# A sequence block with a mixture of experts on one core: VectorE's two products of a block pair, in front of the second scan of a slot

## What is computed

```python
x = x + mamba(layernorm(x))          # in_proj -> conv(4) -> silu -> delta, B, C
                                     # h = h * exp(delta * A) + (delta * xc) * B, per token
                                     # y = sum_n h * C + xc * D;  y * silu(z) @ out_proj
x = x + experts(layernorm(x))        # top 2 of 8: silu(x @ w1) * (x @ w3) @ w2
```

## Time and profile before

| | |
|---|---|
| median of 3 runs | 4781.84 us (4776.21 to 4798.81) |
| the profiled execution: its time | 4794.05 us |
| its span, first to last instruction | 4792.3 us |
| first scan of step 0 | 95.5 us after the span's start |
| steps 0 to 2 end at, tile steps 3 to 14 end at | 518.7 us, 2526.3 us |
| busy in the span: PE, DVE, ACT, POOL | 88%, 52%, 39%, 36% |
| VectorE's products L1213 and L1218 | 91 each, mean 410 and 421 ns |

### The profile page before, as it was taken

The page is one execution under the profiler, slowest core; times in us unless marked ns, Lnnn a source line. Parts: engine busy times, 40 slices in busy tenths (PEclk is TensorE's granted clock), DMA queues, the critical chain, the costliest instruction groups (busy, mean ns, idle before and its releaser), DMA issues. The chain is left out here.

```text
span 4792.3 us, 73789 instructions
## 1 busy us (share of the span) xinstructions
PE 4208.5 (88%) x25764; PEld 3403.0 (71%) x25764; DVE 2471.3 (52%) x3377; ACT 1872.3 (39%) x3912; POOL 1706.9 (36%) x1233
## 2 busy tenths in 40 slices
PE   5777888888887988888887499999999999999999
PEld 4555667666666766666676288887888878888787
DVE  3999988888888888888889300000000000000000
ACT  6676765666566566657655100000000000000000
POOL 3667655665665566466555200000000000000000
PEclk8788989989999989999898699999999999999999
DMA  3112443444344344434433221303030303112210
GB/s 135 67 37 84 139 146 102 150 142 153 108 151 146 102 151 141 156 105 150 146 115 119 88 77 19 102 13 105 14 109 13 105 13 104 18 38 80 82 37 16
DMA packets 289412, 452.63 MB, mean 94 GB/s; under 512 B 15862, under 2 KB 183414, under 8 KB 280822
## 3 DMA queue, kind: packets, MB, share of 16 engines
q1 hardware_dynamic: 273078, 412.71, 26.2%
q0 software_dynamic: 14768, 34.41, 3.8%
q10 hardware_dynamic: 1296, 2.37, 0.1%
HBM read 920.96 MB, written 45.95 MB: 202 GB/s over the span
## 5 line engine op out<-in xcount | busy, mean ns | idle before, releaser
L539 POOL TENSOR_TENSOR hs<-hs,bc 128x1024 f32<-128x1024 f32 x512 | 1218.6, 2381 | 448.6 <-DVE hs L1089 426.8
L1089 DVE TENSOR_TENSOR_SCAN hs<-dA,pU 128x1024 f32<-128x1024 f32 x512 | 1168.6, 2282 | 31.8 <-ACT dA L629 9.8
L629 ACT ACTIVATE dA<-delta,aneg 128x255 f32<-128x255 f32 x2048 | 847.6, 507 | 39.2 <-DVE hs L1089 33.9
L947 PE MATMUL pY<-ident,hs 128*128 128x128 f32 x4096 | 573.6, 293 | 310.3 <-POOL hs L539 310.1
L1514 ACT ACTIVATE gate<-pA 128x512 f32<-128x512 f32 x216 | 117.4, 544 | 1861.0 <-PE pB L1556 1861.0
L1556 PE MATMUL pA<-xT,w1s 128*128 128x128 f32 x6048 | 800.6, 275 | 0.7 <-ACT xT L1527 0.7
L1556 PE MATMUL pB<-xT,w3s 128*128 128x128 f32 x6048 | 799.9, 275 | 0.0
L1429 POOL DMA_INDIRECT out<-ow,trow x54 | 84.4, 1562 | 1971.2 <-DVE ow L1651 1971.2
L947 PEld LDWEIGHTS pY<-ident,hs 128*128 128x128 f32 x4096 | 503.0, 151 | 395.6 <-POOL hs L539 301.9
L1556 PEld LDWEIGHTS pA<-xT,w1s 128*128 128x128 f32 x6048 | 741.8, 192 | 26.4 <-issue 25.3
L1556 PEld LDWEIGHTS pB<-xT,w3s 128*128 128x128 f32 x6048 | 737.3, 192 | 0.0
(11 more groups left out here) (197 smaller groups left out, 3267.1 us busy)
## 6 DMA issues: line engine op xcount, KB each, us to landing
w1s<-in_w SPq DMA_DIRECT2D x165, 1024.0 KB
w3s<-in_w SPq DMA_DIRECT2D x165, 1024.0 KB
w2s<-in_w SPq DMA_DIRECT2D x165, 1024.0 KB
ew<-in_w SPq DMA_DIRECT2D x273, 512.0 KB, 4.4
win<-in_w_in SPq DMA_DIRECT2D x128, 512.0 KB, 3.9
bc<-bc_d SPq DMA_DIRECT2D x64, 1024.0 KB, 11.5
w1s<-in_w SPq DMA_DIRECT2D x55, 512.0 KB
w3s<-in_w SPq DMA_DIRECT2D x55, 512.0 KB
```

Source lines behind the costliest of these rows:

```text
L539: pool.tensor_tensor(hs[b][:, :, :], hs[b][:, :, :], bc[:, N + g * PN:N + (g + 1) * PN, :], ALU.mult)\
L629: e = act.activation(dA[k % NB][:, i, 1:T], delta[:, c, 1:T], ACT.Exp, scale=aneg[:, c, n:n + 1])
L947: m = pe.matmul(pY[c % 2][:, t * P:(t + 1) * P], hs[k % NB][:, i, t * P:(t + 1) * P], ident[:, :], start=g == 0 and i == 0 and t == 0, sto ...
L1089: dve.tensor_tensor_scan(hs[b][:, :, :].rearrange("p n t -> p (n t)"), dA[b][:, :, :].rearrange("p n t -> p (n t)"), pU[:, :, :].rearrange ...
```

## The change

The two products of a block pair, with their waits for the tanh and between each other, are issued at position g = 2 of their slot and not at g = 1. That is one number:

```diff
                 def expert(u, g):
 
                     j = u - UP0 - 1
-                    if 0 <= j < ROUNDS and g == 1:
+                    if 0 <= j < ROUNDS and g == 2:
                         ge(dve, e_tanh, ROUNDS * jt + j + 1)
                         dve.scalar_tensor_tensor(eth[:, :, :], eth[:, :, :], 1.0, pEup[:, 0, :, :], ALU.add, ALU.mult)\
                            .then_inc(e_half, 1)
```

## The result

The changed kernel took 4802.89 us (median of 9 runs, 4790.73 to 4810.71), the kernel before 4786.13 us (9 runs, 4776.21 to 4798.81). The ratio is 1.0028, with a 95% interval of 1.0014 to 1.0041: 13 us slower, 7 to 20. That is under the 0.5% named in the prediction, and outside of zero. The profiled execution took 4802.79 us (span 4801.0).

What follows compares the result with a forecast made beforehand. VectorE bounds steps 0 to 2; in tile steps VectorE and TensorE take turns. Per tile step -0.7 + 2.4 = +1.7 us, times 12 +20 us on the median of 4781.84: 4802 us, range 4776 to 4822.

Steps and rivals of the forecast that it cites:

- the part without the clock: Slot 8, per tile step: at full clock TensorE's next block pair would start 0.7 us earlier.
- the clock term: TensorE after its pause in slot 8: 4.8 us of half clock, 2.4 us lost per tile step.
- Slot 8 carries it all: Only slot 8's moved products cost time; the other slots count 0, with 0.3 us as upper end for slot 7.
- The late products: Slot 8: products wait behind the square root and end 4.9 us later; TensorE stands still for 7.8 us.
- The path behind e8 to L887: Slot 8: ScalarE's table load, tanh and copy, 1.95 us, then the turn of 0.65 us: 2.6 us.
- The table load: ScalarE's load in slot 8's critical piece counted without the skill's drain, which would add 1.3 us, 16 us in sum.
- carried unchanged to the end of the step: The +1.7 us per tile step arising in slot 8 lasts to the step's end, times 12: +20 us.
- L1167 was to wait longer: VectorE's waits at L1145 and L1167 grow by about what the tanh waits lose, plus the step's loss.
- The tanh waits: VectorE's idle for the tanh in the tile steps falls from 84.7 us to about 45, counted as no gain.
- VectorE as the bound: Rival: waits at L1145 and L1167 shrink too in the tile steps; 41 us faster, 4741; chance 0.09.
- The harmless pause: Rival: slot 8's pause costs no clock beyond the old order's loss; 8 us faster, 4774; chance 0.12.
- The slower side: Rival: TensorE's block pair in slot 8 at half clock throughout, loses 3.67 us; 36 us slower, 4818; chance 0.29.

Runs made afterwards that it cites:

- experiment 3: Changed kernel plus 14 unread matmuls on TensorE in slot 8, before its wait for the products, steps 3 to 14: 4780.69 us, 0.9989 of the kernel before.
- the filler of slot 12: Kernel before with the reciprocal moved behind slot 8's second scan, plus 6 unread TensorE matmuls in slot 12: 4717.06 us, ratio 0.9852.
- the filler in slot 0: Kernel before with the reciprocal moved behind slot 8's second scan, plus 14 unread TensorE matmuls in slot 0: 4744.20 us, ratio 0.9912.
- experiment 1: Changed kernel with slot 8's pair of products alone put back at g = 1: 4791.13 us, ratio 1.0000 to the kernel before.

## Why the prediction was right, point by point

**The time.** 4802 was forecast and 4802.89 measured. Part of this closeness is luck: against the 4781.84 us of the first three runs the forecast step is +20 us, and the measured ratio is worth +13, with 7 to 20 in the interval. And the right sum has terms that missed in opposite ways, as the next points show: the part without the clock was put too low, the clock term a little too high, and a gain of 1.1 us later in the step was not seen.

**Slot 8 carries it all.** This is shown from both sides, by the pair put back (1.0000) and by the pair moved alone (1.0040).

**The late products.** The forecast put the end of the products 2.4 us behind the root and the pause at 7.8 us. They are 2.3 us (939.92 to 942.25) and 7.84 us. The path behind e8 to L887 was put at 2.6 us and is 3.1 (947.83 to 950.95): ScalarE's load began 0.3 us after TensorE's end, and the turn took 0.85 us, not 0.65. That is why the sum without the clock came out at -0.7 us and the column to L887 of experiment 3 shows -0.2.

**The clock term.** Half clock for 4.8 us and a loss of 2.4 us were taken from the longest pause. In step 5 it was 3.9 us, and e8 lost 5.53 - 3.67 = 1.9 us; in the mean of the twelve steps it lost 2.2. That this term makes the loss is shown by the filler. The Trainium skill's "TensorE: Matmul & The Clock Gate", Part 1, puts the ramp penalty under 1% of a typical kernel span and advises against fitting a specific count of cold matmuls. The clock behind the pause of slot 8 is worth 0.4% here, within that size, but to leave the term out on that ground would have given no loss at all. The prediction read more into it than it says: that sentence of the Trainium skill is on the warm-up at a kernel's start, and its Part 1 counts the cost each time where pauses recur.

**The table load.** The load at 948.10 took 1.28 us, and the tanh began 1.29 us after its start: no drain of 1.38 us stands behind it, as in the earlier trace rows, and the tanh begins 1.56 us after TensorE's end of e8, so none stands ahead of it either. The Trainium skill's "ScalarE: Activation LUTs", section "What ACT_TABLE_LOAD costs", gives 1.28 us for the load and 1.38 for the drain, 2.66 for a switch. The trace agrees with the first and not with the sum.

**What failed** is half of one step: "carried unchanged to the end of the step". It was carried to L701 except for 0.2 us, but the stretch from L701 to L1167 took 15.78 us instead of 16.90. The projection behind the pause at the turn is the place, in step 5:

```profile
994.35 1.22 PE L932 MATMUL pY<-xc,skip 128*128 128x256 f32 x2 [3.16 <-ACT ysum L641]
...
995.79 4.43 PE L827 MATMUL pM<-xnT,win 128*128 128x256 f32 x16
```

The same 16 matmuls took 5.93 us before, behind a pause of the same 3.16 us. In the mean of the twelve steps they took 5.34 us before and 4.23 after, which is the 1.1 us. The half clock lasted less long. With the filler of slot 12 the stretch is 15.14 us, so the half clock cost 1.8 us in it before and 0.6 after. Why it was shorter stays open. In steps 4 to 13 of the changed kernel it goes with e8: in the six steps where e8 took 5.30 to 5.76 us the projection took 4.33 to 4.56, and in the four where e8 took 6.27 to 6.29 it took 3.62, which is full clock throughout. In the kernel before there is no such link. The stretch is short in the four kernels whose products of slot 8 stand at g = 2 (15.78, 15.99, 16.02, 16.10) and long in the three with g = 1 and no filler (16.90, 16.63, 16.70; with the filler in slot 0 it is 16.35), but each has one profile, and no run here tells a cause. It goes with the one waiting time that went against the forecast: L1167 was to wait longer, and waits 6.7 us instead of 17.9.

**The tanh waits** fell to 63.8 us and not to about 45. Slot 5 (13.5 us in the twelve steps, then 0) and most of slot 10 (18.1, then 3.7) went as worked out. The wait of slot 11 was to lose 1.4 us a step and grew instead, from 49.8 to 54.9 us, in step 5 from 3.69 to 5.24 where 2.3 was expected. One part of that is e10 itself, which ran partly at half clock in six of the twelve steps (in three of the kernel before):

```profile
966.24 0.66 PE L913 MATMUL pS<-ident,xb 128*128 128x128 f32 x4 [0.84 <-ACT xnT L695]
966.71 5.36 PE L810 MATMUL pE<-xf,ew 128*128 128x128 f32 x32
```

In step 5 it took 3.57 us to the next work before (956.84 to 960.41) and 5.20 here (966.71 to 971.91); the granted clock over these stretches is 1.00 and 0.67. The rest is that e10 starts later against VectorE's scans, 3.18 us behind the start of the last one before it (963.53) where it was 1.70 (955.14 to 956.84). The prediction had counted neither. With slot 8's pair put back (experiment 1), where e10 takes 3.57 us throughout, the tanh waits are 48.8 us, near the forecast. As the wait of slot 11 is hidden, it cost the sum nothing.

**The rivals.** VectorE as the bound is out (experiment 1). The harmless pause is out as it stands, and would be true without the clock (experiment 3). The slower side, e8 at half clock throughout, would make e8 7.3 us; it took up to 6.29 in single steps and 5.86 in the mean.

## What to carry to other kernels

When an operation is moved on an in-order engine, look at what it now stands behind, not only at what it stands in front of: here one of seven moved pairs slid behind a wait for ScalarE, and so held TensorE. The wait that hurt was for a value not needed until a slot later, and moving that wait was worth 1%, over three times what the change cost. And a pause of TensorE on its critical path has a price beyond its length, in the clock that it is granted afterwards; useless matmuls in the pause are a quick test of whether it is paid. Behind the pause of slot 0, in most steps the longest, it was not.

## What the runs showed of the hardware

- The half clock behind a pause of 3.16 us cost 0.5% of this kernel (0.9900 to 0.9852 with six useless matmuls a step in the pause), the one behind a pause of 7.8 us in slot 8 about 0.4% (1.0028 to 0.9989), and the one behind 8.8 us in slot 0 nothing that can be told (0.9900 to 0.9912). Here it was not the length of the pause that decided but what ran behind it: in slot 0 VectorE was the later engine.
- The same pause of 3.16 us, in the same place of the twelve tile steps, was followed by 16 matmuls of 4.60 to 5.99 us in the kernel before and of 3.62 to 5.94 us in the changed one; at full clock they take 3.62. A price read from one pause in one step can be off by more than 1 us.
- Single profiles of two kernels differed by 4.3 us in steps that are the same in both. Differences of a few tenths of a per cent were readable in stretches of a step, and not in the span.
